# Probabilities times values ahead of the first and fifth pair of heads in a fused decoder layer (self attention, cross attention, routed experts)

## The reference, cut to what matters

```
x = layernorm(x + self_attention(x))                    # 32 sequences, 256 tokens, width 256, 16 heads of 16, rotary
x = layernorm(x + cross_attention(x, ctx, ctx, mask))   # same sizes, biases, mask by key, output projection
x = layernorm(x + experts(x))                           # 8 experts, hidden 1024, top 2, capacity 1.25, gelu

# one attention:
scores = q @ k.T / 4 ; attn = softmax(scores) ; out = attn @ v
```

## Time and profile before

| | |
|---|---|
| median of 3 runs | 2276.23 us (2272.47 to 2283.42) |
| the profiled execution | 2272.46 us |
| its span | 2270.7 us |
| mean granted clock of TensorE | 0.963 of full speed |
| PE busy | 2169.6 us, 96% |
| DVE, ACT, GpSimd (POOL) busy | 1180.0, 1007.8, 648.9 us |

### The profile page before, as it was taken

One profiled execution on the slowest core, in us unless ns is written; L12 is line 12 of the kernel. 1 busy time (PEld: TensorE's weight loads), 2 busy tenths in 40 slices (PEclk: granted clock), 3 DMA queues, 4 the chain that ended last, 5 costly groups with the idle time before them and its releaser, 6 DMA issues. The chain is left out here.

```text
span 2270.7 us, 48602 instructions
## 1 busy us (share of the span) xinstructions
PE 2169.6 (96%) x18846; PEld 1509.7 (66%) x18846; DVE 1180.0 (52%) x2458; ACT 1007.8 (44%) x1538; POOL 648.9 (29%) x1001
## 2 busy tenths in 40 slices
PE   8999999999999999999999999999799999999990
PEld 4566666666666666666666666666478778787780
DVE  3466666766766766667676676764111111111114
ACT  1355555555555555555555555553231222212225
POOL 2112323333233332333323333222312122121223
PEclk6799999999999999999999999998799999999995
DMA  6301111111101111001010010100113331333217
GB/s 181 102 21 30 44 31 49 53 42 51 51 27 31 37 30 29 22 26 33 25 30 22 28 33 24 28 20 14 37 35 84 77 71 32 82 84 77 24 17 303
DMA packets 97667, 115.72 MB, mean 51 GB/s; under 512 B 12097, under 2 KB 91022, under 8 KB 95393
## 3 DMA queue, kind: packets, MB, share of 16 engines
q1 hardware_dynamic: 68112, 82.38, 11.5%
q0 software_dynamic: 17664, 18.35, 5.1%
q10 hardware_dynamic: 11664, 11.88, 1.8%
HBM read 64.53 MB, written 56.05 MB: 53 GB/s over the span
## 5 line engine op out<-in xcount | busy, mean ns | idle before, releaser
L867 DVE TENSOR_REDUCE smax<-ps_s 128x4 f32<-128x1024 f32 x500 | 610.0, 1220 | 352.3 <-PE ps_s L574 286.3
L753 ACT ACTIVATE prob<-ps_e 128x1024 f32<-128x1024 f32 x500 | 512.3, 1025 | 524.5 <-PE ps_e L583 427.4
L574 PE MATMUL ps_s<-stack 17*128 17x256 f32 x4000 | 574.1, 404 | 24.9 <-DVE smax L867 9.8
L583 PE MATMUL ps_e<-stack 18*128 18x256 f32 x4000 | 574.7, 405 | 5.6 <-DMA stack<-nrows 3.9
L574 PEld LDWEIGHTS ps_s<-stack 17*128 17x128 f32 x4000 | 350.6, 186 | 206.6 <-issue 97.7
L583 PEld LDWEIGHTS ps_e<-stack 18*128 18x128 f32 x4000 | 345.7, 186 | 11.4 <-DMA stack<-nrows 5.9
L1543 ACT ACTIVATE hid<-m_ps_h,b_sb 128x320 f32<-128x320 f32 x256 | 135.0, 527 | 415.7 <-PE m_ps_h L1503 411.5
L1503 PE MATMUL m_ps_h<-m_cols,w_sb 128*128 128x320 f32 x1024 | 293.3, 436 | 0.6 <-DVE m_cols L1560 0.6
L1520 PE MATMUL m_ps_o<-w_sb,hid 128*128 128x256 f32 x1280 | 278.9, 379 | 0.0
L1520 PEld LDWEIGHTS m_ps_o<-w_sb,hid 128*128 128x128 f32 x1280 | 243.2, 190 | 34.8
L599 PE MATMUL ps_w<-prob,val 128*32 128x256 f32 x4096 | 257.3, 393 | 1.3 <-ACT prob L753 1.3
(11 more groups left out here) (134 smaller groups left out, 2270.8 us busy)
## 6 DMA issues: line engine op xcount, KB each, us to landing
w_sb<-in_w SPq DMA_DIRECT2D x16, 1024.0 KB, 6.5
slot_rows_dram<-fill ACTq DMA_DIRECT2D x8, 1290.0 KB, 9.7
m_rows<-slot_rows_dram SPq DMA_DIRECT2D x16, 645.0 KB, 4.5
xT<-in_xT SPq DMA_DIRECT2D x32, 256.0 KB, 2.8
ctxT<-in_ctxT SPq DMA_DIRECT2D x32, 256.0 KB, 2.8
x_res<-in_x SPq DMA_DIRECT2D x32, 256.0 KB, 2.9
stack<-nrows SPq DMA_DIRECT2D x512, 2.0 KB
sums_dram<-x SPq DMA_DIRECT2D x32, 256.0 KB
```

What stands on the lines that cost most here:

```text
L574: mm = nc.tensor.matmul(scores[:, p % 2, t, :], stack[X][rows, Q, p // HG, t * P:(t + 1) * P], stack[X][rows, K, p // HG, :], start=True, ...
L583: mm = nc.tensor.matmul(shifted[:, p % 2, t, :], stack[Y][rows, K, h // HG, t * P:(t + 1) * P], stack[Y][rows, Q, h // HG, :], start=True, ...
L753: nc.scalar.activation(prob[:, h:h + 2, :].rearrange("p h s -> p (h s)"), shifted[:, :, :, :].rearrange("p h t s -> p (h t s)"), ACT.Exp, ...
L867: nc.vector.tensor_reduce(max_columns(X, p), scores[:, :, :, :], AX.X, ALU.max)\
```

## The change

On PE `duo` is issued behind `with_values` at m = 0 and m = 4, where it was issued ahead of it. On ACT the copy `out_columns` at m = 0 and m = 4 is issued ahead of the exponential of that duo, where it was behind it. No instruction is added or removed, and no other engine's program changes.

```diff
@@ block.tensor, emit
             for m in range(DUOS):
-                duo(X, bX, Y, bY, m)
                 if m == 0 and there(bX - 1):
                     with_values(X, bX - 1, 1)
                 elif m == DUOS // 2 and there(bY):
                     with_values(Y, bY, 0)
+                duo(X, bX, Y, bY, m)
@@ block.scalar, emit
-                if there(bY):
-                    exponentials(Y, bY, m, shift_tile(X, bX, Y, bY, m))
                 if m == 0 and there(bX - 1):
                     out_columns(X, bX - 1, 1)
                 elif m == DUOS // 2 and there(bY):
                     out_columns(Y, bY, 0)
+                if there(bY):
+                    exponentials(Y, bY, m, shift_tile(X, bX, Y, bY, m))
```

## The result

The changed kernel takes 2541.12 us, the median of four runs (2523.48 to 2548.70), against 2275.12 us for the kernel before (2272.47 to 2283.42): a ratio of 1.1154, 95% interval 1.1123 to 1.1184, 262 us more. 2547 us was predicted. The profiled execution took 2523.48 us, the shortest of the four; its span is 2521.7 us, 251 us more than before, so this trace shows the change at its mildest.

What follows compares the result with a forecast made beforehand. PE was taken to bound the attention pipeline, busy 396.45 of 400 us. Gaps +158, the vanished wait -9 and the clock +122 gave +271 us on 2276.2, so 2547 us, range 2420 to 2630.

Steps and rivals of the forecast that it cites:

- The gaps: Behind the first and fifth duo PE idles until the tiles are free: 91 x 1.45 and 30 x 0.87 us, +158 us.
- the wait that goes: At the first duo of a CROSS half step, PE's wait for ACT's stack copy goes: -9 us.
- The clock: In steady steps the new gaps bring PE's clock down: 30 steps x 1.2 falls x 3.4 us lost, +122 us.
- somewhat under half of the three large ones: Reason for 1.2 clock falls a step: steady steps have three gaps of 1.4 us, of which under half bring a fall.
- The Trainium skill's rule: Only idle gaps longer than any of the new ones bring PE's clock down; the sum would stay at +149 us.
- with_values' own wait: Ahead of m = 0 and m = 4 it needs the previous duo's exponential; costed at nothing, 9 us if ACT came late.
- L599 waits for the exponential: Sign of being wrong: `with_values` waits on PE for ACT, instead of following L501 directly; the sum is then too low.
- ACT's exchange: At m = 0 and m = 4 the 0.58 us `outT` copy lies under the duo, so the exponential is not delayed: nothing.
- The sum: For the whole kernel, +149 us without the clock and +122 us for it: +271 us, 2547 us.
- the held clock: Rival: the gaps come, but `values` and `with_values` ahead of the duo keep PE's clock up; 2425 us, chance 0.18.
- constant falls: Rival: PE's clock falls at nearly every large gap, +306 us for the clock; 2731 us, chance 0.05.
- the faster one: Rival: stack copy hidden, next duo's tiles free if reduction and exponential end within 1.08 us; 2267 or 2263 us, chance 0.02.

Runs made afterwards that it cites:

- the dummy matmuls: The changed kernel with bfloat16 matmuls whose result nobody reads put into the new gaps on PE: 2447.95 us beside 2270, ratio 1.0781.
- the one of the other chip: The changed kernel itself run once more, on another chip, against the kernel before: 2536.39 us beside 2256.01, ratio 1.1254.
- two gaps a step: The kernel before with only the exchange at m = 0 made, on PE and ACT, m = 4 left as before: ratio 1.0742.
- ACT's order alone: The kernel before with only the ACT part of the change, PE still running `with_values` behind the duo: ratio 1.1060.
- PE alone: The kernel before with only the PE part of the change, ACT keeping the exponential ahead of the copy of `outT`: ratio 1.1172.

## Why the prediction was right

**The gaps** were forecast at 91 of 1.45 and 30 of 0.87 us, 158 us; measured 152 us, on chips where the wait that goes (-9 us) does not exist. By the waits in the trace after it is 147. Their places, number and length came out as written: 1.37 us of idle PE against 1.38 in the earlier trace rows, three a step, and one of 0.78. The one half step of the old trace in which two duos stood side by side was enough to price them.

**The clock** was the term with the weakest ground: 122 us forecast, 131 measured on the one kind of chip and at least 84, with the falls that the dummy matmuls left some 100, on the other. I took 1.2 falls a step of 6.8 us; the trace after has 35 in the 30 steps, of 5.8 us, and the one of the other chip 46 of 5.9. The size holds, the reason given for it does not: "somewhat under half of the three large ones" counts a fall for a gap, but with two gaps a step there were 47 falls in the steady part, the one at 1022.60 came without a large gap ahead of it, and the longer gaps of ACT's order alone brought only 18. That the number came out near was partly luck.

The Trainium skill's rule ("TensorE: Matmul & The Clock Gate", HAM oscillation) would have left the sum at 149 us; the falls in this trace and the 84 us that the dummy matmuls gave back speak against it for gaps this short.

**with_values' own wait** was costed at nothing, with 9 us if ACT came late in the place with the thinnest cover. The prediction named as a sign of being wrong that "L599 waits for the exponential (then ACT is late, and the sum is too low)", and on the chip of the forecast this was met: 10.7 us for `with_values` and 10.0 for duos from 200 to 1550 us, some 26 in 30 steps. The wait came at m = 0, where the cover was thick, since the eighth duo's signals are late there. The trace before had it, as a wait for the stack copy, of which I read the releaser and not the cause. On the other chips the step held.

**The wait that goes**, -9 us, is such a signal too: it exists on the first kind of chip alone.

**ACT's exchange** at nothing: shown, for PE alone gives the same time.

**The sum** of 271 us against 262 is thus better than its terms. On the chip of the forecast the gaps were some 6 to 11 us below it, the waits for ACT some 26 above, and the clock some 20 to 30 below. The rivals of the held clock (2425 us) and of constant falls (2731) are both out, and the faster one met its condition nowhere.

## What to carry to other kernels

When a group of instructions is moved from between two users of a single tile, look for the place in the trace where those users already stand side by side: the start-to-start time there, less that of now, is the price of each place. On PE a gap can cost twice, as idle time and by the clock: here 152 us and 84 to 131 us. How much the clock adds cannot be told from the idle time, so it is to be read from the granted clock of a run. A wait in one profile may belong to the chip: before building on it, see whether it is there on a second one.

## What the runs showed that was not expected

The clock's price is not in proportion to the gaps: 208 us at the low level with two gaps a step, 184 and 253 with four, and 61 with four mostly longer ones behind `with_values`. A fall can come after a stretch in which PE was busy 2.97 of 3.40 us.

On some chips DVE and ACT start 1.1 to 2.6 us after the eighth duo of a SELF half step, mostly some 1.2 us after the end of one of POOL's indirect DMA instructions; on others the same program has nothing of it, and they start at most 0.5 us after a duo that they waited for. Whether the DMAs have a part in it on the first kind was not tried, since the kernels without them ran on the second. Worth 7.3 us of PE waits in the kernel before, it may be part of the 13 to 18 us between the medians of the two kinds of chip.
